# GpSimd makes three of the eight high parts of the activations in the gate

## The chip, the cores and the metric

The kernel runs on one core of one Trainium2 chip. The metric is the device time of one execution in microseconds. Engines are called PE (TensorE), DVE (VectorE), ACT (ScalarE), POOL (GpSimd) and SP (the queue that issues most DMAs).

## The reference

A graph network with two convolutions is followed by a mixture-of-experts layer over 6250 rows of 256 values. Only the second part matters here:

```
x = layernorm(x)
H = gelu(x @ W1 + b1)                       # 6250 x 1024
probs = softmax(H @ Wg + bg)                # 8 experts
assign = argmax(probs)
out = x_in + probs[e] * (H @ Wd[e] + bd[e]) # with e = assign, row by row
```

## The kernel before

The rows are cut into 49 tiles of 128, and two tiles make a pair. The work runs in stages with a barrier between them: sorting the edges, aggregation, two linear layers, aggregation again, the end of the graph network, then the **gate** and the **experts**. The gate computes H and the eight logits for each pair, picks an expert for each row, counts each row's place among those of its expert, and scatters the row to that place in a table in HBM. The experts stage reads the table back in order, computes H once more, and multiplies by the weights of the chosen expert.

Products are made in float16 with every operand split into a high and a low part. The 1024 hidden units are 8 chunks `h` of 128. In the gate every pair `i` (steps 0 to 24, the last with one tile) goes through this:

- PE (`pe_hidden`): six matmuls of 256 columns for each chunk, into one of four PSUM banks (`UB = 4`). Chunk `h` waits until the GELU of four chunks earlier has read the bank (`u.gelu`). After chunk 1 it transposes the rows of the next pair out of `stage`; after chunk 4 it makes the `ranks` of pair i-3, which wait for `s_slot` of pair i-4. After the eight chunks come the `logits` of pair i-1 (32 small matmuls).
- ACT (`act_hidden`): GELU of each chunk into `hf` (one buffer for the eight chunks, so the GELU of chunk `h` also waits until `h_lo` of that chunk of the pair before has been made, `u.split`). It makes the high part `h_hi` of chunks 0, 2, 3, 5 and 7, each one behind the GELU of the next chunk, and after `h_hi` of chunk 2 the high part of the next pair's transposed rows (`xt_hi`).
- DVE (`dve_hidden`): for chunks 1, 4 and 6 (`DVE_HIGH`) `h_hi` as well (L1920), and for all eight the low part `h_lo = hf * beta - h_hi` (L1925), in the order of the chunks. After chunk 0 comes `place` for pair i-4 (L2148 to L2153, gives `slot`), after chunk 3 `xt_lo` (L1907), which the next pair's first matmul waits for, and `choose` for pair i-2 (L2128 to L2139).
- POOL: for each i a copy of the pair's rows into `stage` (L2037), as soon as PE has transposed pair i-2 (`u.tr`), and then the two scatters (L2042) of pair i-6, as soon as DVE has placed it.

Steps 4 to 21 of PE, ACT and DVE run in a hardware loop of two steps; the others and all of POOL are written out. The order on each engine is that of the code; semaphores alone join the engines. After the last step DVE finishes the places of the last four pairs, works out which rows each tile of the experts stage has, and SP writes padding rows and the probabilities; then comes the barrier. `dve_hidden` serves the experts stage too.

Of the kernel before, what the change touches and what calls it, by code (L numbers as in the profile page):

```python
# [20 lines left out]
ALU = mybir.AluOpType  # L21
AX = mybir.AxisListType

P = 128
N, C, IC, HID, NEXP, NE = 6250, 256, 512, 1024, 8, 100000
EPS = 1e-5
NT = -(-N // P)
NP_ = NT * P
LAST = N - (NT - 1) * P
KC, KI, KH = C // P, IC // P, HID // P  # L30
# [220 lines left out]
def prepare(nc, m, a):  # L251
# [5 lines left out]
    EARLY = [(NBUILT + 6 * q, NBUILT + 6 * q + 6) for q in range(NADJ // 6)]  # L257
    LATE = [(0, 6), (6, 12), (12, NBUILT)]
    COUNTS = EARLY + LATE
    assert NADJ % 6 == 0 and NBUILT - 12 <= 7  # L260
# [1553 lines left out]
UB = 4  # L1814
DVE_HIGH = (1, 4, 6)
# [88 lines left out]
def dve_xt(dve, m, u, i, par, ntile):  # L1904
    i = i + u.first
    dve.wait_ge(u.xthi, i + 1)
    dve.tensor_tensor(m.xt_lo[:, par, :, 0:ntile * P],  # L1907
                      m.ps[:, TBANK, :].rearrange("p (k n) -> p k n", k=KC)[:, :, 0:ntile * P],
                      m.xt_hi[:, par, :, 0:ntile * P], ALU.subtract).then_inc(u.xt, 1)


def dve_hidden(dve, m, u, i, par, ntile, nxt, between={}):

    n = ntile * P
    i = i + u.first
    highs = 0
    for h in range(KH):
        if h in DVE_HIGH:
            dve.wait_ge(u.gelu, i * KH + (h + 1 + UB))
            dve.tensor_scalar(m.h_hi[:, par, h, 0:n], m.hf[:, h, 0:n], m.beta[:, h:h + 1], None, ALU.mult).then_inc(u.own, 1)  # L1920
            dve.wait_ge(u.own, i * len(DVE_HIGH) + (DVE_HIGH.index(h) + 1))
        else:
            highs += 1
            dve.wait_ge(u.hi, i * (KH - len(DVE_HIGH)) + highs)
        dve.scalar_tensor_tensor(m.h_lo[:, par, h, 0:n], m.hf[:, h, 0:n], m.beta[:, h:h + 1], m.h_hi[:, par, h, 0:n],  # L1925
                                 ALU.mult, ALU.subtract).then_inc(u.split, 1)
        if h == 3 and nxt:
            dve_xt(dve, m, u, i + 1 - u.first, 1 - par, nxt)
        if h in between:
            between[h]()  # L1930
# [19 lines left out]
def gate(nc, m, a):  # L1950

    rows = m.rows
# [8 lines left out]
    rk, slotf, slot = take("rk", [P, 2, NEXP], F32), take("slotf", [P, 2], F32), take("slot", [P, NT], I32)  # L1961
# [3 lines left out]
    stage = take("stage", [P, 2, 2, C], F32)  # L1965
# [6 lines left out]
    u = m.hidden  # L1972
# [8 lines left out]
    NPAIR = NT // 2  # L1981
    LB, RB = (5, 7), 6
    tiles = lambda i: 1 if i == NPAIR else 2
# [11 lines left out]
    with nc.Block() as block:  # L1995
        @block.sync
        def _(sp):
            for e in range(0, NEXP, 2):
                n = KH // 2
                sp.dma_start(m.wd[:, e:e + 2, :, :, :, :].rearrange("p e k h t c -> p (e k) (h t c)"),  # L2000
                             m.wd_dram[e * n:(e + 2) * n, :, :].rearrange("n p f -> p n f")).then_inc(m.s_wd, 16)
            sp.dma_start(m.bd[:, :, :].rearrange("p e c -> p (e c)"), bass.AP(a.fbd.tensor, 0, [[0, P], [1, NEXP * C]])).then_inc(m.s_bd, 16)
            sp.wait_ge(s_const, 8)
            sp.dma_start(m.sorted_rows[NEXP * REG:NEXP * REG + P, :], prow[:, :]).then_inc(s_padded, 16)
            sp.wait_ge(s_pads, 1)
            for e in range(NEXP):
                at = sp.value_load(padi[0:1, e:e + 1], min_val=e * REG, max_val=e * REG + NP_)
                sp.dma_start(m.sorted_rows[bass.ds(at, P), :], prow[:, :]).then_inc(s_padded, 16)
            sp.wait_ge(s_probS, 1)
            sp.dma_start(m.prob_dram.rearrange("(t p) c -> t (p c)", p=P), probT[:, :]).then_inc(m.s_prob, 16)  # L2010
            sp.wait_ge(s_padded, 16 * (NEXP + 1))

        @block.gpsimd
        def _(pool):
            pool.iota(rows[:, :, C].bitcast(I32), [[P, NT]], base=0, channel_multiplier=1).then_inc(s_const, 1)
            pool.memset(tri[:, :], 1.0).then_inc(s_init, 1)
            pool.memset(prow[:, :], 0.0).then_inc(s_init, 1)
            pool.memset(valid[:, :], 1.0).then_inc(s_init, 1)
            pool.wait_ge(s_init, 3)

            pool.affine_select(out=tri[:, :], in_=tri[:, :], compare_op=ALU.is_ge, fill=0.0,
                               base=-1, pattern=[[1, P]], channel_multiplier=-1).then_inc(s_const, 1)
            pool.affine_select(out=valid[:, :], in_=valid[:, :], compare_op=ALU.is_ge, fill=0.0,
                               base=LAST - 1, pattern=[[0, 1]], channel_multiplier=-1).then_inc(s_const, 1)
            pool.iota(prow[:, C:C + 1].bitcast(I32), [[0, 1]], base=N, channel_multiplier=0).then_inc(s_const, 1)
            pool.iota(prio[:, :], [[-1, NEXP]], base=NEXP, channel_multiplier=0, allow_small_or_imprecise_dtypes=True).then_inc(s_const, 1)
            for t in (run, m.reg_base):
                pool.iota(t[:, :], [[REG, NEXP]], base=0, channel_multiplier=0, allow_small_or_imprecise_dtypes=True).then_inc(s_const, 1)
            pool.iota(tv[:, :], [[1, 64]], base=0, channel_multiplier=0, allow_small_or_imprecise_dtypes=True).then_inc(s_const, 1)
            pool.wait_ge(s_const, 8)  # L2030
            LATE = 6
            for i in range(NPAIR + 1 + LATE):
                if i <= NPAIR:
                    n = tiles(i)
                    if i >= 2:
                        pool.wait_ge(u.tr, i - 1)
                    pool.tensor_copy(stage[:, i % 2, 0:n, :], rows[:, 2 * i:2 * i + n, 0:C]).then_inc(s_stage, 1)  # L2037
                if i >= LATE:
                    pool.wait_ge(s_slot, i - LATE + 1)
                    for t in range(2 * (i - LATE), 2 * (i - LATE) + tiles(i - LATE)):  # L2040
                        n = P if t < NT - 1 else LAST
                        pool.indirect_dma_start(m.sorted_rows, bass.IndirectOffsetOnAxis(ap=slot[:n, t:t + 1], axis=0),  # L2042
                                                rows[:n, t, :], None).then_inc(s_scat, 16)
            pool.wait_ge(s_scat, 16 * NT)

        @block.tensor
# [64 lines left out]
        def _(dve):  # L2111
# [29 lines left out]
            def place(dve, i, par, ntile):  # L2141
                t = slice(0, ntile)

                def lk(ins, n):
                    ins.then_inc(s_place, 1)
                    dve.wait_ge(s_place, i * 4 + n)
                dve.wait_ge(s_rk, i + 1)
                lk(dve.tensor_tensor(rk[:, t, :], m.ps[:, RB, 0:NEXP * ntile].rearrange("p (t e) -> p t e", e=NEXP),  # L2148
                                     run[:, :].unsqueeze(1).to_broadcast([P, ntile, NEXP]), ALU.add), 1)
                lk(dve.tensor_tensor(rk[:, t, :], rk[:, t, :], ohf[:, par, t, :], ALU.mult), 2)  # L2150
                lk(dve.tensor_tensor(run[:, :], run[:, :], m.ps[:, RB, 2 * NEXP:3 * NEXP], ALU.add), 3)
                lk(dve.tensor_reduce(slotf[:, t], rk[:, t, :], AX.X, ALU.add), 4)
                dve.tensor_copy(slot[:, bass.ds(2 * i, ntile)], slotf[:, t]).then_inc(s_slot, 1)  # L2153

            def step(dve, i, par, n):
                nxt = 0 if n == NPAIR else 1 if n == NPAIR - 1 else 2

                between = {}
                if n is None or n >= 4:
                    between[0] = lambda: place(dve, i - 4, par, 2)  # L2160
                if n is None or n >= 2:
                    between[3] = lambda: choose(dve, i - 2, par, 2)
                dve_hidden(dve, m, u, i, par, 1 if n == NPAIR else 2, nxt, between)
            dve_xt(dve, m, u, 0, 0, 2)
            steps(dve, step)
            for i in range(NPAIR - 3, NPAIR + 1):
                place(dve, i, i % 2, tiles(i))
# [208 lines left out]
```

## Time and profile before

| | us |
|---|---|
| median of 3 runs | 1857.0 |
| lowest and highest | 1855.56 and 1859.79 |
| time of the profiled execution | 1859.56 |
| its span in the profile | 1857.8 |
| gate, from its first POOL work to its last scatter | 1297 to 1515 |
| experts stage | from about 1525 |

The profile gives, for each engine, when each instruction ran and what ended the wait before it. The granted clock of PE is shown as a share of its full rate. "x3" means that three instructions are merged into one row, whose duration is that of all three; those of an engine overlap a little.

### The profile page before, as it was taken

How to read it: one execution, taken by the hardware profiler on the slowest of the kernel's cores; microseconds unless marked ns; L12 is line 12 of the kernel's file. 1: busy time of each engine (PE TensorE's matmuls, PEld its weight loads, DVE VectorE, ACT ScalarE, POOL GpSimd, SP SyncE). 2: the span in 40 equal slices, each digit the busy share in tenths (PEclk: the TensorE clock that was granted, in tenths of full speed). 3: DMA queues.
4: the chain of work that ended last, by engine and by line, in shares of the span. 5: the costliest groups of instructions: out<-in, count | busy, mean ns of one | idle time of the engine just before them, and what ended most of it. 6: DMA issues, size and time to landing. Idle time of an engine off the chain costs nothing. (4 is left out here: it accounts for less than half of the span.)

```text
span 1857.8 us, 36775 instructions
## 1 busy us (share of the span) xinstructions
PE 1579.0 (85%) x11153; PEld 1182.1 (64%) x11154; DVE 1178.6 (63%) x4511; ACT 971.2 (52%) x2001; POOL 936.2 (50%) x989
## 2 busy tenths in 40 slices
PE   0229999999999896989999999975888839999996
PEld 0215666666666696856656555655777728899995
DVE  6478888888886377932234344337788965656663
ACT  0555555555554355832334222228888837766773
POOL 5747677777777000047777777723133332333433
PEclk9999999999999897999999999989999969999998
DMA  8546566666666000478999999837500021111110
GB/s 248 164 138 214 193 208 208 209 208 208 209 208 208 12 0 32 148 260 309 299 314 313 336 321 313 291 122 231 195 34 34 32 75 33 48 47 46 48 47 15
DMA packets 152562, 305.72 MB, mean 165 GB/s; under 512 B 26099, under 2 KB 107989, under 8 KB 144638
## 3 DMA queue, kind: packets, MB, share of 16 engines
q1 hardware_dynamic: 104354, 191.99, 29.6%
q0 software_dynamic: 41744, 105.90, 18.1%
q10 hardware_dynamic: 6348, 6.40, 1.1%
q8 instruction: 58, 0.95, 0.2%
q14 instruction: 58, 0.48, 0.1%
HBM read 212.02 MB, written 99.68 MB: 168 GB/s over the span
## 5 line engine op out<-in xcount | busy, mean ns | idle before, releaser
L1165 POOL DMA_INDIRECT grows<-table_dram,gsrc x680 | 657.9, 967 | 337.3 <-issue 309.0
L1099 PE MATMUL ps<-table,adj 128*128 128x512 f16 x2842 | 707.1, 381 | 5.7 <-PEq L1466 5.7
L1099 PEld LDWEIGHTS ps<-table,adj 128*128 128x128 f16 x2842 | 389.7, 142 | 169.3 <-issue 12.1
L856 ACT ACTIVATE adj<-ps 128x490 f16<-128x490 f32 (+1 forms) x390 | 223.5, 573 | 182.3 <-PE ps L841 178.2
L1893 ACT ACTIVATE hf<-ps,b1f,unscale 128x256 f32<-128x256 f32 (+1 forms) x424 | 233.4, 562 | 119.6 <-PE ps L1864 95.8
L1864 PE MATMUL ps<-xt_hi,fw_parts 128*128 128x256 f16 (+1 forms) x1696 | 255.4, 274 | 5.5 <-DVE xt_lo L1907 5.3
L828 DVE TENSOR_SCALAR oh_k<-iota_k,keyrem 128x246 f16<-128x246 f16 x780 | 237.8, 309 | 0.0
L1925 DVE SCALAR_TENSOR_TENSOR h_lo<-hf,beta,h_hi 128x256 f16<-128x256 f32 (+1 forms) x424 | 190.1, 482 | 70.0 <-ACT h_hi L1888 64.3
L827 DVE TENSOR_SCALAR oh_r<-iota_r,keyrem 128x128 f16<-128x128 f16 x780 | 214.9, 278 | 26.6 <-PE ps L841 21.6
L1048 PE MATMUL ps<-grows,oh_g 128*128 128x512 f16 x680 | 167.1, 380 | 18.0 <-DMA grows<-table_dram,gsrc 18.0
L1864 PEld LDWEIGHTS ps<-xt_hi,fw_parts 128*128 128x128 f16 x1696 | 162.4, 98 | 26.2 <-DVE xt_lo L1907 5.4
L841 PE MATMUL ps<-oh_k,oh_r 128*128 128x245 f16 x780 | 148.7, 273 | 17.3 <-DVE oh_k L828 13.6
L1864 PE MATMUL ps<-xt_lo,fw_parts 128*128 128x256 f16 (+1 forms) x848 | 162.3, 273 | 0.0
L2276 PE MATMUL ps<-wd,h_hi 128*128 x896 | 148.4, 273 | 0.9 <-DVE y L2333 0.9
L841 PEld LDWEIGHTS ps<-oh_k,oh_r 128*128 128x128 f16 x780 | 75.6, 98 | 94.8 <-DVE oh_k L828 20.2
L1888 ACT ACTIVATE h_hi<-hf,beta 128x256 f16<-128x256 f32 (+1 forms) x265 | 133.0, 502 | 1.7
L920 DVE SCALAR_TENSOR_TENSOR tmp_d<-ps,disP,tmp_d 128x256 f32<-128x256 f32 x30 | 14.5, 484 | 186.6 <-ACT tmp_d L1124 186.6
L913 DVE TENSOR_SCALAR oh_g<-iota_r,gloc 128x128 f16<-128x128 f16 x680 | 125.7, 281 | 0.3
L1048 PEld LDWEIGHTS ps<-grows,oh_g 128*128 128x128 f16 x680 | 65.4, 98 | 93.3 <-DMA grows<-table_dram,gsrc 23.9
L2255 POOL DMA_INDIRECT out<-out_rows,in_rows x56 | 57.3, 1023 | 130.3 <-DVE out_rows L2337 121.8
L2276 PE MATMUL ps<-wd,h_lo 128*128 x448 | 122.1, 273 | 0.0
L2042 POOL DMA_INDIRECT sorted_rows<-rows,slot x49 | 48.5, 989 | 128.6 <-DVE slot L2153 121.0
(354 smaller groups left out, 2228.8 us busy)
## 6 DMA issues: line engine op xcount, KB each, us to landing
adj_dram<-adj SPq DMA_DIRECT2D x30, 1568.0 KB
adj<-adj_dram SPq DMA_DIRECT2D x30, 1568.0 KB, 8.2
cv_raw<-fwd SPq DMA_DIRECT2D x64, 256.0 KB, 5.5
table_dram<-table SPq DMA_DIRECT2D x14, 896.0 KB, 4.1
grows<-table_dram,gsrc POOLq DMA_INDIRECT x680
wd_dram<-cv_parts SPq DMA_DIRECT2D x32, 256.0 KB, 5.1
wd<-wd_dram SPq DMA_DIRECT2D x4, 2048.0 KB, 16.8
in_rows<-sorted_rows SPq DMA_DIRECT2D x56, 129.5 KB, 2.1
```

The costliest lines, as they stand in the source:

```text
L827: dve.tensor_scalar(a.oh_r[:, n % OHR, i, :], m.iota_r[:, :], m.keyrem[:, 1, j, w:w + 1], None, ALU.is_equal)
L828: last = dve.tensor_scalar(a.oh_k[:, n % OHR, i, :], m.iota_k[:, :], m.keyrem[:, 0, j, w:w + 1], None, ALU.is_equal)
L841: last = pe.matmul(m.ps[:, n % 3, at:at + keys], a.oh_r[:, n % OHR, i, :], a.oh_k[:, n % OHR, i, 0:keys], start=True, stop=True)
L856: act.activation(m.adj[:, q % 3, d0:d0 + wide, :].rearrange("r d c -> r (d c)"), m.ps[:, n % 3, 0:wide * NT], ACT.Copy).then_inc(a.s_adj, 1)
L1048: last = pe.matmul(acc, m.oh_g[:, n % GOR, j, :], m.grows[:, n % GR, j, :], start=False, stop=part == PT - 1 and j == PARTS[part] - 1)
L1099: last = pe.matmul(acc, adj[:, :, c], table[:, c, :], start=c == 0, stop=c == NT - 1)
L1165: pool.indirect_dma_start(m.grows[:, n % GR, j, :], None, m.table_dram, bass.IndirectOffsetOnAxis(ap=m.gsrc[:, g, part * BT + j:part * BT ...
L1864: last = pe.matmul(m.ps[:, h % UB, 0:n], m.w1[:, 2 * k + half, w, at:at + P], x[:, par, k, 0:n], start=q == 0 and k == 0, stop=q == 2 and ...
L1888: act.activation(m.h_hi[:, par, h, 0:n], m.hf[:, h, 0:n], ACT.Copy, scale=m.beta[:, h:h + 1]).then_inc(u.hi, 1)
L1893: act.activation(m.hf[:, h, 0:n], m.ps[:, h % UB, 0:n], ACT.Gelu, bias=m.b1f[:, h:h + 1], scale=m.unscale[:, 0:1]).then_inc(u.gelu, 1)
L1925: dve.scalar_tensor_tensor(m.h_lo[:, par, h, 0:n], m.hf[:, h, 0:n], m.beta[:, h:h + 1], m.h_hi[:, par, h, 0:n], ALU.mult, ALU.subtract).th ...
L2276: last = pe.matmul(m.ps[:, DB + j, 0:C], h[:, par, k, j * P:(j + 1) * P], w, start=q == 0 and k == 0, stop=q == 2 and k == KH - 1)
```

## The change

DVE no longer makes `h_hi` of chunks 1, 4 and 6 in the gate. POOL makes them, with the same instruction, and raises the same semaphore `u.own` that DVE's `h_lo` already waits on. POOL's order becomes, for step i: high part of chunk 1, first scatter of pair i-6, high part of chunk 4, second scatter, high part of chunk 6, copy of the rows of pair i+2. Each high part waits for its GELU and for the logits of pair i-2 (`u.done`), whose buffer it overwrites. The copies no longer wait for `u.tr` when they are the first two, and those of pair i+2 come behind step i's last high part. After step 24 POOL has the scatters of pairs 19 to 24 left. The experts stage is unchanged.

```diff
-def dve_hidden(dve, m, u, i, par, ntile, nxt, between={}):
+def dve_hidden(dve, m, u, i, par, ntile, nxt, between={}, pool_high=False):
...
         if h in DVE_HIGH:
-            dve.wait_ge(u.gelu, i * KH + (h + 1 + UB))
-            dve.tensor_scalar(m.h_hi[:, par, h, 0:n], m.hf[:, h, 0:n], m.beta[:, h:h + 1], None, ALU.mult).then_inc(u.own, 1)
+            if not pool_high:
+                dve.wait_ge(u.gelu, i * KH + (h + 1 + UB))
+                dve.tensor_scalar(m.h_hi[:, par, h, 0:n], m.hf[:, h, 0:n], m.beta[:, h:h + 1], None, ALU.mult).then_inc(u.own, 1)
             dve.wait_ge(u.own, i * len(DVE_HIGH) + (DVE_HIGH.index(h) + 1))
...
+            def copy(i):
+                n = tiles(i)
+                if i >= 2:
+                    pool.wait_ge(u.tr, i - 1)
+                pool.tensor_copy(stage[:, i % 2, 0:n, :], rows[:, 2 * i:2 * i + n, 0:C]).then_inc(s_stage, 1)
+
+            def high(i, h):
+                n = tiles(i) * P
+                pool.wait_ge(u.gelu, i * KH + (h + 1 + UB))
+                pool.wait_ge(u.done, i + 1)
+                pool.tensor_scalar(m.h_hi[:, i % 2, h, 0:n], m.hf[:, h, 0:n], m.beta[:, h:h + 1], None, ALU.mult).then_inc(u.own, 1)
+
+            def scatter(t):
+                n = P if t < NT - 1 else LAST
+                pool.indirect_dma_start(m.sorted_rows, bass.IndirectOffsetOnAxis(ap=slot[:n, t:t + 1], axis=0),
+                                        rows[:n, t, :], None).then_inc(s_scat, 16)
+
+            for i in range(2):
+                copy(i)
             for i in range(NPAIR + 1 + LATE):
-                if i <= NPAIR:
-                    n = tiles(i)
-                    if i >= 2:
-                        pool.wait_ge(u.tr, i - 1)
-                    pool.tensor_copy(stage[:, i % 2, 0:n, :], rows[:, 2 * i:2 * i + n, 0:C]).then_inc(s_stage, 1)
-                if i >= LATE:
-                    pool.wait_ge(s_slot, i - LATE + 1)
-                    for t in range(2 * (i - LATE), 2 * (i - LATE) + tiles(i - LATE)):
-                        n = P if t < NT - 1 else LAST
-                        pool.indirect_dma_start(...).then_inc(s_scat, 16)
+                for k in range(len(DVE_HIGH)):
+                    if i <= NPAIR:
+                        high(i, DVE_HIGH[k])
+                    if i >= LATE and k < tiles(i - LATE):
+                        pool.wait_ge(s_slot, i - LATE + 1)
+                        scatter(2 * (i - LATE) + k)
+                if i + 2 <= NPAIR:
+                    copy(i + 2)
```

## Rows read from the trace of the kernel before

**Rows 1.** Busy us (count) of PE, PEld, DVE, ACT, POOL, and clock, in one stretch.

```profile
1345.55:1476.37 130.82, 109.61 (x1430) 96.31 (x1428) 116.70 (x417) 109.32 (x224) 41.19 (x49) 1.00 0.09 33
```

**Rows 2.** Waits in that stretch: who for whom, total us, times, longest.

```profile
PE ps L2066 <- DVE slot L2153: 23.1, 17, 1.9
```

**Rows 3.** DVE in order of time, one pair.

```profile
1401.36 0.17 DVE L2148 TENSOR_TENSOR rk<-ps,run 128x16 f32<-128x16 f32 x1
...
1402.28 0.17 DVE L2153 CAST slot<-slotf 128x2 f32 x1
1402.41 0.35 DVE L1920 TENSOR_SCALAR h_hi<-hf,beta 128x256 f16<-128x256 f32 x1
1402.80 1.28 DVE L1925 SCALAR_TENSOR_TENSOR h_lo<-hf,beta,h_hi 128x256 f16<-128x256 f32 x3
1403.99 0.68 DVE L1907 TENSOR_TENSOR xt_lo<-ps,xt_hi 128x512 f16<-128x512 f32 x1
...
1405.33 0.33 DVE L2131 TENSOR_TENSOR now<-now,mx 128x16 f32<-128x16 f32 x1
...
1409.60 0.17 DVE L2148 TENSOR_TENSOR rk<-ps,run 128x16 f32<-128x16 f32 x1
```

**Rows 4.** ACT in order of time, the same pair and the next.

```profile
1403.58 1.14 ACT L1893 ACTIVATE hf<-ps,b1f,unscale 128x256 f32<-128x256 f32 x2 [0.42 <-PE ps L1864]
...
1406.35 1.22 ACT L1893 ACTIVATE hf<-ps,b1f,unscale 128x256 f32<-128x256 f32 x2 [0.24 <-PE ps L1864]
1407.47 0.50 ACT L1888 ACTIVATE h_hi<-hf,beta 128x256 f16<-128x256 f32 x1
...
1410.54 0.51 ACT L1888 ACTIVATE h_hi<-hf,beta 128x256 f16<-128x256 f32 x1
```

**Rows 5.** PE in order of time: the ranks, and the next transposes.

```profile
1402.51 0.18 PE L2066 MATMUL ps<-oh,tri 128*128 128x8 f16 x1 [1.11 <-DVE slot L2153]
...
1406.73 0.60 PE L1850 MATMUL ps<-id,stage 128*128 128x128 f32 x4
```

**Rows 6.** POOL in order of time, scatters of the first and last pair of the stretch.

```profile
1345.55 0.99 POOL L2042 DMA_INDIRECT sorted_rows<-rows,slot  x1 [5.59 <-DVE slot L2153]
1346.84 0.96 POOL L2042 DMA_INDIRECT sorted_rows<-rows,slot  x1 [0.30 <-issue]
...
1476.37 0.98 POOL L2042 DMA_INDIRECT sorted_rows<-rows,slot  x1 [5.36 <-DVE slot L2153]
```

**Rows 7.** POOL's groups by line and shape, whole span (busy us, mean ns, idle).

```profile
L1598 POOL TENSOR_TENSOR rs<-ve,mh 128x4 f32<-128x4 f32 x12 | 12.1, 1006 | 38.8 <-DVE ve L1637 38.8
L380 POOL CAST words<-dst_i 100x1024 int16<-100x1024 int32 x1 | 1.3, 1317 | 3.6 <-DMA dst_i<-dst 3.6
L2037 POOL COPY stage<-rows 128x256 f32<-128x256 f32 x1 | 0.4, 409 | 0.0
```

**Rows 8.** POOL in order of time, two copies near the gate's start.

```profile
1312.53 0.79 POOL L2037 COPY stage<-rows 128x512 f32<-128x512 f32 x1 [7.08 <-PE ps L1850]
...
1326.02 0.61 POOL L2037 COPY stage<-rows 128x512 f32<-128x512 f32 x1 [5.96 <-PE ps L1850]
```

**Rows 9.** DVE in order of time around those two copies.

```profile
1311.97 0.88 DVE L1925 SCALAR_TENSOR_TENSOR h_lo<-hf,beta,h_hi 128x256 f16<-128x256 f32 x2
...
1326.11 1.19 DVE L1925 SCALAR_TENSOR_TENSOR h_lo<-hf,beta,h_hi 128x256 f16<-128x256 f32 x2
```

**Rows 10.** DVE in order of time: places of steps 4 and 24, the last high part.

```profile
1335.57 0.17 DVE L2148 TENSOR_TENSOR rk<-ps,run 128x16 f32<-128x16 f32 x1
...
1497.87 0.17 DVE L2148 TENSOR_TENSOR rk<-ps,run 128x16 f32<-128x16 f32 x1
...
1502.74 0.28 DVE L1920 TENSOR_SCALAR h_hi<-hf,beta 128x128 f16<-128x128 f32 x1
```

**Rows 11.** POOL's last scatter of the gate.

```profile
1513.11 1.57 POOL L2042 DMA_INDIRECT sorted_rows<-rows,slot  x1 [0.31 <-issue]
```

**Rows 12.** SP's queue at the gate's end, the padding rows.

```profile
1512.69 9.34 SPq L2008 DMA_DIRECT2D sorted_rows<-prow  x8
```

More of the change, by code:

```diff
@@ L2031, in _ @@
             LATE = 6
-            for i in range(NPAIR + 1 + LATE):
-                if i <= NPAIR:
-                    n = tiles(i)
-                    if i >= 2:
-                        pool.wait_ge(u.tr, i - 1)
-                    pool.tensor_copy(stage[:, i % 2, 0:n, :], rows[:, 2 * i:2 * i + n, 0:C]).then_inc(s_stage, 1)
-                if i >= LATE:
-                    pool.wait_ge(s_slot, i - LATE + 1)
-                    for t in range(2 * (i - LATE), 2 * (i - LATE) + tiles(i - LATE)):
-                        n = P if t < NT - 1 else LAST
-                        pool.indirect_dma_start(m.sorted_rows, bass.IndirectOffsetOnAxis(ap=slot[:n, t:t + 1], axis=0),
-                                                rows[:n, t, :], None).then_inc(s_scat, 16)
+            def copy(i):
[14 more added lines that the diff above has]
+                copy(i)
+            for i in range(NPAIR + 1 + LATE):
+                for k in range(len(DVE_HIGH)):
[6 more added lines that the diff above has]
+                    copy(i + 2)
             pool.wait_ge(s_scat, 16 * NT)
@@ L2162, in step @@
                     between[3] = lambda: choose(dve, i - 2, par, 2)
-                dve_hidden(dve, m, u, i, par, 1 if n == NPAIR else 2, nxt, between)
+                dve_hidden(dve, m, u, i, par, 1 if n == NPAIR else 2, nxt, between, pool_high=True)
             dve_xt(dve, m, u, 0, 0, 2)
```

## Prediction

> **What bounds the kernel now.** The change touches the gate alone, so I looked first for what sets the length of a step there. The view of busy time by stretch, over the regular part of the gate, is the start. DVE is busy 116.7 of 130.82 us, ACT and PE 109 each, POOL 41 [rows 1]. The stretch runs from the first scatter of one pair to that of the pair 16 later, so a step takes 130.82 / 16 = 8.18 us [rows 6]. PE's granted clock is 1.00 in it, the 2.4 GHz level.
>
> The view of waits says who is late: PE waits 17 times, 23.1 us in all, for DVE's `slot` before its ranks [rows 2]. ACT's waits are for PE's chunks behind these ranks: it stands 0.42 and 0.24 us in one step [rows 4]. DVE's own order of time then shows one pair from `place` to `place`, 1401.36 to 1409.60, 8.24 us, in which it waits for no other engine's data [rows 3]. The reader is to see that DVE is the engine that everything else follows here. POOL has 5.4 to 5.6 us in each step in which it waits for `slot` [rows 6], so it has time for more.
>
> **What the change removes.** One `h_hi` on DVE takes from 1402.41 to the start of the next instruction at 1402.80, 0.39 us [rows 3]. Three a step are 1.17 us. DVE's own step without them is 8.24 - 1.17 = 7.07 us.
>
> That isn't yet the new step, since loops through several engines come next. I work them out from the same pair:
>
> - The ranks loop. Ranks at 1402.51 on PE [rows 5]; PE's chunks 5 to 7, logits and chunks 0 and 1 follow, and the GELU of the next chunk 1 ends at 1406.35 + 1.22 = 1407.57, 5.06 us on. ACT's `h_hi` of chunk 0 ends at 1407.97, 0.40 later [rows 4]. Then on DVE `h_lo` of chunk 0, 0.40 with some 0.08 of signalling (three take 1402.80 to 1403.99), and `place`, 1401.36 to 1402.45, 1.09 [rows 3], and 0.06 to the next ranks. The sum is 7.09 us a step.
> - The longer loop, over two steps. Up to that GELU again 5.06. ACT then ends `h_hi` of chunk 3 at 1411.05, 3.48 us on [rows 4]. DVE does `h_lo` of chunk 3, 0.48 with the signalling, and from `xt_lo` at 1403.99 to the next `place` at 1409.60 another 5.61, of which the change removes 2 x 0.39, so 4.83. `place` and the way to the ranks are 1.15 [rows 3]. The sum is 5.06 + 3.48 + 0.48 + 4.83 + 1.15 = 15.00 us, 7.50 a step.
>
> So without any cost of POOL's new work the step would be 7.50 us, not 7.07.
>
> **What POOL's work costs.** No row shows this instruction on POOL. The nearest one is POOL's copy of 128x256 f32, 409 ns: the same elements, one tensor read. The cast of 1024 int32 took 1317 ns, 1.3 ns an element with all of its fixed cost; 256 elements at that and a fixed 0.2 us are 0.53. The dearest row of an arithmetic operation there is 1006 ns, for four elements, which is a power and not a product [rows 7]. I take 0.41 us, keep 0.41 below and 1.0 above; it is nearest to the copy. POOL's step is then 3 x 0.41 + 2 x 0.97 + 0.30 + 0.62 = 4.1 us of 7.5, and 5.9 with the upper price. Its time hides beside the others unless one of its results is late:
>
> - The high parts. That of chunk 1 starts when the GELU of chunk 1 is done, as ACT's of chunk 0 does, and DVE has `h_lo` of chunk 0 and the whole `place` to do before it needs it. Those of 4 and 6 start while DVE is still at chunk 3, `xt_lo` and `choose`. A scatter ahead of one holds it up by at most 0.97 + 0.30. Covered; if the cover were gone, it would cost DVE up to 1.3 us a step.
> - The copy for pair i+2, behind the high part of chunk 6. The GELU of chunk 6 ends at 1403.58 + 1.14 = 1404.72 [rows 4] and PE comes to the transposes at 1406.73 [rows 5], 2.0 us later. High part and copy take 0.41 + 0.62 = 1.03, with signals and the end of a scatter up to 1.6. Covered by 0.4 us; with the price of 1.0 it is late by about 0.2. Pairs 2 and 3 lose the early copies they have now; I put down 0.3 us in all for the filling of the pipeline.
> - The scatters. They move two steps later and no longer wait for `slot`. After POOL's last high part (DVE's was at 1502.74 [rows 10]) 11 are left, 11 x 1.27 = 14.0 us, so they end near 1517.1 on the old axis, where the last now ends at 1514.7 [rows 11]. SP's eight padding rows last until 1522.0 [rows 12]. Hidden, with 4.9 us for the last rows to land.
>
> **What the two engines cost each other.** A copy on POOL began at 1326.02, `h_lo` on DVE at 1326.11, and two `h_lo` took 1.19 us where two took 0.88 at 1311.97 [rows 8, 9]: DVE stood 0.31 us, until 0.40 after the copy's start. The copy that began behind a running `h_lo` at 1312.53 took 0.79 in place of 0.61 [rows 8]. In `choose`, `now` took 0.33 beside a copy [rows 3]. So the one that comes second stands. The copy has 512 elements and held DVE for 0.40; a high part has 256, so 0.20 by an estimate from those rows. `h_lo` is eight times 0.40 us of a step. I take it that three high parts and the moved copy hold DVE for some 0.3 us more in two steps of the longer loop (between none and 4 x 0.2 a step), 0.15 a step. The step is 7.65 us.
>
> The Trainium skill (page "SBUF — State Buffer", section "Who interferes with whom") says that a VectorE instruction with two SBUF inputs and a GpSimd instruction that reads SBUF exclude each other, and that the second is blocked until the first is done. That speaks against this change, since `h_lo` reads `hf` and `h_hi`. The trace agrees that DVE stands, but for 0.40 us of a copy that is 0.61 long, not for all of it [rows 8, 9]. By the rule as it stands each high part could cost DVE its full 0.41, three 1.23 against the 1.17 removed, and the time would be 1857 in place of the 1847 below.
>
> **The sum.** The steps that shorten are those between the places of steps 4 and 24: 1335.57 to 1497.87, 20 steps, 8.115 us on average [rows 10]. They save 20 x (8.115 - 7.65) = 9.3 us. Step 24's three high parts of 128 columns (0.28 each) leave DVE's path too, 0.8, less 0.1 of standing. Start of the pipeline: -0.3. Together 9.7 us. Against the profiled execution that is 1859.56 - 9.7 = 1849.9; the median of the runs shown is 2.6 below it, so 1857.0 - 9.7 = 1847.3, say **1847**.
>
> **The rivals.**
> - The ranks loop alone bounds (7.1 us a step): the longer loop overlaps better than I lay it out, and POOL's reads fall where DVE reads PSUM. For it speaks that POOL's high part of chunk 1 runs beside ACT's of chunk 0, when DVE mostly waits. 20 x 1.0 + 0.7 = 20.7 us: 1836.
> - No change: each high part holds DVE as long as it was there itself, 3 x 0.39, because nearly every one meets a running `h_lo` and the handing over costs as much again as the reading. The work has then only moved: 1857. The rule of "SBUF — State Buffer" in the Trainium skill would end here too. Against it stands the 0.40 of a copy twice as long.
> - Slower, by one mechanism: POOL's product is dear (1.0 us, which the power in rows 7 allows). Less the fixed 0.2 us it then holds DVE for 0.8, 2.4 a step if all three meet `h_lo`. With half of them the step is 7.50 + 1.2 = 8.7, 20 x (8.7 - 8.115) = 12 us more in all: 1869. The point from which it decides: DVE stands more than 8.115 - 7.50 = 0.6 us a step longer in the longer loop, or 0.2 for each high part with every one meeting `h_lo`.
> - The change doesn't free DVE since `h_lo` of chunks 1, 4, 6 now waits for POOL in place of doing the work: possible if DVE keeps up with ACT closely; same size as no change, and taken with it.
>
> **How the numbers follow.** Forecast (step 7.4 to 7.9, 1842 to 1852): 0.55. Ranks loop alone, around 1836: 0.13. Between forecast and no change, and no change, 1853 to 1861: 0.18. Slower: 0.14. A measurement of this kernel tells apart 0.2%, 3.7 us, so faster below 1853.3: 0.55 + 0.13 + a part of the third case, 0.04 = 0.72; same 0.14; slower 0.14. The range leaves out the top of the slow case and the best of the fast one: 1836 to 1859.
>
> **What would show it.** Right: no L1920 on DVE before 1500, 75 new ones on POOL near 0.41 us; scatters apart by 7.65 us; PE's wait for `slot` smaller than 1.1 us a step; some `h_lo` longer than 0.48 beside POOL's instructions; copies ended before PE asks, no wait of the transposes for `stage`; scatters after the last step back to back and no wait of SP or the experts for them. Wrong: POOL's high part above 0.6 us, DVE waiting for `h_hi` of POOL, or PE's transposes waiting for POOL.

## The result, and the profile after

The changed kernel takes 1852.22 us (median of 8 runs, 1850.44 to 1858.72), the kernel before, measured beside it, 1859.76 us. The ratio is 0.9967 with a 95% interval of 0.9953 to 0.9982: 0.33%, some 6 us, with between 3.3 and 8.7 us possible. The two medians lie 7.5 us apart, inside that interval; one of the eight runs of the kernel before took 5939.86 us, and the ratio leaves it out. The forecast was 9.7 us, outside the interval. The direction was right and 1852 lies in the range, but the size was forecast too large. Of the 5.2 us between 1847 and 1852.2, 2.8 have nothing to do with the change: the kernel before itself took 1859.76 us beside the changed one, and not the 1857.0 that the forecast started from.

The profiled execution took 1853.08 us, 6.5 less than the 1859.56 of before. Where they went is read from five times in each trace: the first instruction of the gate on VectorE (the `memset` of `ones`), the places of step 4, of step 24 and the last, and SyncE's first load of the next stage, the experts.

| stretch, us | before | after | difference | forecast |
|---|---|---|---|---|
| gate's start to place of step 4 | 39.04 | 39.29 | +0.25 | +0.3 |
| 20 steps | 162.30 | 153.90 | -8.4 | -9.3 |
| step 24 to the last place | 12.79 | 12.33 | -0.46 | -0.7 |
| last place to the experts' first load | 14.60 | 17.22 | **+2.6** | 0 |
| gate in all | 228.73 | 222.74 | -6.0 | -9.7 |

What lies outside the gate differs by -0.5 us and is no part of the change. So the steps and step 24 came out near the forecast, and the term that stood at nothing cost 2.6 us. The start's +0.25 can't be told from nothing: two more traces of the changed kernel have 39.0 and 38.6 us there, and a second trace with the gate of before (price, below) has 39.3.

VectorE in order of time, around the places of steps 4 and 24 [rows 10] and the last:

```profile
1336.24 0.16 DVE L2166 TENSOR_TENSOR rk<-ps,run 128x16 f32<-128x16 f32 x1
...
1490.14 0.16 DVE L2166 TENSOR_TENSOR rk<-ps,run 128x16 f32<-128x16 f32 x1
...
1502.47 0.17 DVE L2166 TENSOR_TENSOR rk<-ps,run 128x8 f32<-128x8 f32 x1 [0.38 <-PE ps L2089]
```

(1490.14 - 1336.24) / 20 = 7.695 us a step, where it was 8.115. Away from the loop's ends, over the 14 steps in its middle, it is 7.80 where it was 8.18; I call that the regular step.

Busy time in the regular part (the columns of [rows 1], a slightly shorter stretch), and its waits (total, times, longest; [rows 2]):

```profile
1345.55:1470.00 124.45, 111.10 (x1422) 95.15 (x1420) 108.92 (x368) 109.21 (x224) 93.59 (x95) 1.00 0.09 32
```

```profile
PE ps L2084 <- DVE slot L2171: 13.1, 16, 1.0
...
ACT hf L1893 <- PE ps L1864: 6.7, 24, 0.4
DVE h_lo L1926 <- ACT h_hi L1888: 4.2, 15, 0.6
...
PEld ps L1850 <- POOL stage L2038: 2.4, 8, 0.3
```

VectorE is no longer alone at the top: PE has 89% of the stretch, ACT and VectorE 88% each, where it was 84% for PE and ACT and 89% for VectorE. PE's wait for `slot` fell from 1.4 us a time to 0.8. VectorE now waits for ACT's `h_hi` of chunk 3, the link of the longer loop. And POOL went from 31% to 75% busy, 5.9 us a step where the forecast had 4.1. Its groups by shape say why (busy us, mean ns, idle before), against [rows 7]:

```profile
L2044 POOL TENSOR_SCALAR h_hi<-hf,beta 128x256 f16<-128x256 f32 x72 | 77.0, 1069 | 56.0 <-ACT hf L1893 55.1
...
L2048 POOL DMA_INDIRECT sorted_rows<-rows,slot x49 | 50.7, 1035 | 9.8 <-issue 8.8 <-DVE slot L2171 0.9
```

The product takes 1.07 us on average, not 0.41. POOL and VectorE in order of time show what it does to its neighbour ([rows 3] has VectorE's before). In `choose`, `now` is the logits less their greatest, `lg` a copy of that, and `sc` and `ohf` mark the expert that is picked:

```profile
1400.10 0.92 POOL L2044 TENSOR_SCALAR h_hi<-hf,beta 128x256 f16<-128x256 f32 x1 [0.38 <-ACT hf L1893]
...
1402.26 0.94 POOL L2044 TENSOR_SCALAR h_hi<-hf,beta 128x256 f16<-128x256 f32 x1
1403.14 0.60 POOL L2038 COPY stage<-rows 128x512 f32<-128x512 f32 x1
1404.55 1.35 POOL L2044 TENSOR_SCALAR h_hi<-hf,beta 128x256 f16<-128x256 f32 x1 [0.80 <-ACT hf L1893]
```

```profile
1400.42 0.48 DVE L1926 SCALAR_TENSOR_TENSOR h_lo<-hf,beta,h_hi 128x256 f16<-128x256 f32 x1 [0.26 <-ACT h_hi L1888]
...
1402.16 0.17 DVE L2149 TENSOR_TENSOR now<-now,mx 128x16 f32<-128x16 f32 x1
1402.59 0.64 DVE L2151 COPY lg<-now 128x16 f32 x1 [0.26 <-DVE now L2149]
1403.11 0.16 DVE L2152 SCALAR_TENSOR_TENSOR sc<-now,prio 128x16 f32<-128x16 f32 x1
...
1403.51 0.27 DVE L2154 TENSOR_TENSOR ohf<-sc,best 128x16 f32<-128x16 f32 x1
...
1403.92 2.21 DVE L1926 SCALAR_TENSOR_TENSOR h_lo<-hf,beta,h_hi 128x256 f16<-128x256 f32 x5
1406.05 0.16 DVE L2166 TENSOR_TENSOR rk<-ps,run 128x16 f32<-128x16 f32 x1
...
1410.49 0.59 DVE L2152 SCALAR_TENSOR_TENSOR sc<-now,prio 128x16 f32<-128x16 f32 x1
```

POOL's high part of chunk 6 (1402.26 to 1403.20) falls into `choose`. The copy `lg`, 0.17 us long elsewhere, takes 0.64 and ends at 1403.23, just as POOL is done; one step on it is `sc` that takes 0.59. The high part of chunk 1 comes second, behind a running `h_lo`, and there POOL is the one that is held up: 1.35 us in place of 0.92. The high part of chunk 4 (1400.10 to 1401.02) has a whole `h_lo` of VectorE beside it (1400.42 to 1400.90), and neither is longer than elsewhere, 0.92 and 0.48. So the same instruction has three outcomes in one step, by where it falls.

The end of the gate is a block's end: every engine drains its queues and then all meet at a barrier. SyncE's and POOL's rows there (how long in ns, when), before and then after:

```profile
L1995 POOLq DRAIN  x1: 4071/4071/4071, 1519.9 to 1519.9; - x1
...
L1995 SPq DRAIN  x1: 7/7/7, 1524.1 to 1524.1; - x1
L1995 SPq EVENT_SEMAPHORE  x1: 17/17/17, 1524.3 to 1524.3; - x1
```

```profile
L1996 POOLq DRAIN  x1: 4071/4071/4071, 1514.5 to 1514.5; - x1
...
L1996 SPq DRAIN  x1: 7/7/7, 1516.2 to 1516.2; - x1
L1996 SPq EVENT_SEMAPHORE  x1: 17/17/17, 1518.7 to 1518.7; - x1
```

Before, POOL's drain ended at 1519.9 + 4.07 = 1523.97 and SyncE was ready at 1524.1: a tie. After, SyncE is ready at 1516.2 and all wait for POOL until 1518.6. The last scatters [rows 11, 12] in the changed kernel:

```profile
1507.48 1.57 POOL L2048 DMA_INDIRECT sorted_rows<-rows,slot  x1 [0.30 <-issue]
```

```profile
1504.42 9.84 SPq L2009 DMA_DIRECT2D sorted_rows<-prow  x8
```

The last place came 8.2 us earlier and the last scatter only 5.6. From its end at 1509.05 to the drain's start are 5.4 us for its rows to land, and 4.07 more for the drain: 9.5 us in which the forecast counted 4.9.

### The profile page after: what moved, and what is told of

Read it like the earlier page. It is cut to its first block and busy times, and to the rows that moved or that the text cites. A ratio compares the mean times of both kernels' runs of the same rounds, so it can differ in the third digit from the quotient of the medians.

```text
span 1851.3 us, 36796 instructions
## 1 busy us (share of the span) xinstructions
PE 1586.4 (86%) x11153; PEld 1184.4 (64%) x11154; DVE 1165.9 (63%) x4436; ACT 971.2 (52%) x2001; POOL 1015.1 (55%) x1064
## 5 line engine op out<-in xcount | busy, mean ns | idle before, releaser
L2044 POOL TENSOR_SCALAR h_hi<-hf,beta 128x256 f16<-128x256 f32 (+1 forms) x75 | 79.6, 1062 | 56.9 <-ACT hf L1893 56.0
```

## The experiments

Three questions: what the product costs by itself and what of that reaches the step; which instructions stand for which; and whether the end really costs 2.6 us. Most kernels were timed against the kernel before on the same chip. All regular steps, and "last place to load", are from the traces, as above. The regular step repeats well: three traces of the changed kernel have 7.80, 7.80 and 7.81, three with the scatters a step nearer 7.80 each, the two of act6 7.59 and 7.58.

| kernel | regular step | last place to load | ratio to before |
|---|---|---|---|
| before | 8.18 | 14.60 | 1 |
| changed | 7.80 | 17.22 | 0.9967 (0.9953 to 0.9982) |
| plain_copy | 7.74 | 17.81 | 0.9949 (0.9929 to 0.9968) |
| none_made | 7.51 | 16.59 | 0.9927 (0.9905 to 0.9948) |
| moved_only | 8.04 | 16.32 | 1.0013 (0.9992 to 1.0034) |
| two_tensors | 8.01 | 16.49 | 1.0028 (0.9981 to 1.0074) |
| late5 | 7.80 | 15.44 | 0.9971 (0.9926 to 1.0016) |
| copy_first | 7.86 | 17.85 | 0.9971 (0.9923 to 1.0019) |
| both14 | 7.82 | 14.74 | 1.0010 (0.9968 to 1.0051) |
| no_read | 7.62 | 18.02 | one run, 2118.8 beside 2131.0 |
| act6 | 7.59 | 14.69 | 0.9946 (0.9910 to 0.9982) |
| after_again (changed) | 7.80 | 17.70 | 0.9983 (0.9948 to 1.0017) |
| late5_again | 7.80 | 16.04 | 0.9941 (0.9908 to 0.9973) |
| after_third (changed) | 7.81 | 17.47 | 0.9966 (0.9953 to 0.9979) |
| late5_third | 7.80 | 14.91 | 0.9967 (0.9954 to 0.9980) |
| act6_again | 7.58 | 14.52 | 0.9922 (0.9904 to 0.9939) |

two_tensors to both14, and then no_read, act6, after_again and late5_again, ran where the stages ahead of the gate took far longer (the kernel before 2121 us beside the first four and 2131 us beside the others). The gate's own steps are comparable, the ratios of these are loose. "Last place to load" is less so: in all of them SyncE came to the barrier after POOL (in after_again 16.6 us after the last place against POOL's 16.2, in late5_again 14.9 against 13.3), so there it doesn't show POOL's drain.

**price**: the kernel before, with single instructions on POOL behind its scatters, each waited for, nothing beside them.

```diff
             pool.wait_ge(s_scat, 16 * NT)
+            pool.wait_ge(u.tr, NPAIR + 1)
+            pool.wait_ge(s_probS, 1)
+            for n in (128, 256, 512):
+                alone(pool.tensor_copy(to32, src))
+                alone(pool.tensor_copy(to16, src))
+                alone(pool.tensor_scalar(to32, src, m.beta[:, 1:2], None, ALU.mult))
+                alone(pool.tensor_scalar(to16, src, m.beta[:, 1:2], None, ALU.mult))
+                alone(pool.tensor_scalar(to16, src, 0.5, None, ALU.mult))
+            alone(pool.tensor_tensor(low[:, 1, 0, 0:256], src, m.beta[:, 1:2].to_broadcast([P, 256]), ALU.mult))
```

> The kernel before, with 16 added instructions on GpSimd at the end of the gate, one at a time with nothing beside them; they write buffers that nobody reads any more. They give the price of a product by a column of scalars and of its neighbours. Theory A (the product itself is dear on GpSimd): the product of 128x256 f32 to f16 takes 0.85 to 0.95 us alone, twice the copy's 0.41. Theory B (it takes the copy's 0.41 alone, and in the gate it is stretched by VectorE's reads of two tensors): 0.41 to 0.5 us alone. The time of the whole is of no interest here; it should be some 10 us above the kernel before.

POOL in order of time:

```profile
1525.26 0.53 POOL L2063 TENSOR_SCALAR stage<-rows 128x128 f16<-128x128 f32 x1
1525.85 0.40 POOL L2059 COPY stage<-rows 128x256 f32<-128x256 f32 x1
1526.31 0.40 POOL L2060 CAST stage<-rows 128x256 f16<-128x256 f32 x1
...
1527.83 0.92 POOL L2062 TENSOR_SCALAR stage<-rows,beta 128x256 f16<-128x256 f32 x1
1528.84 0.85 POOL L2063 TENSOR_SCALAR stage<-rows 128x256 f16<-128x256 f32 x1
...
1532.79 1.56 POOL L2062 TENSOR_SCALAR stage<-rows,beta 128x512 f16<-128x512 f32 x1
...
1536.01 0.61 POOL L2065 TENSOR_TENSOR stage<-rows,beta 128x256 f16<-128x256 f32 x1
```

The product of 128x256 takes 0.92 us with nothing beside it, the copy and the cast 0.40. From 256 to 512 elements it grows by 0.64, that is 2.5 ns an element, where the copy has 0.8. The type written makes no difference, the column of scalars 0.07. The same product written with two tensors takes 0.61. The price of 0.41 was too small by more than twice, and most of it, 0.92 of the 1.07, is the instruction itself and not its neighbour.

**plain_copy**: POOL's high part is a plain cast of `hf`; `beta` is left out of it. **none_made**: POOL makes no high part at all, it only raises the semaphore; `h_hi` of chunks 1, 4 and 6 stays at the zero written once at the start.

```diff
 # plain_copy
-                pool.tensor_scalar(m.h_hi[:, i % 2, h, 0:n], m.hf[:, h, 0:n], m.beta[:, h:h + 1], None, ALU.mult).then_inc(u.own, 1)
+                pool.tensor_copy(m.h_hi[:, i % 2, h, 0:n], m.hf[:, h, 0:n]).then_inc(u.own, 1)
 # none_made
-                pool.tensor_scalar(m.h_hi[:, i % 2, h, 0:n], m.hf[:, h, 0:n], m.beta[:, h:h + 1], None, ALU.mult).then_inc(u.own, 1)
+                pool.sem_inc(u.own, 1)
```

> The changed kernel with a copy to f16 in place of GpSimd's product; the factor beta is left out of the high parts of chunks 1, 4 and 6, everything else is as it was. If the dear product is what keeps the gate's step at 7.8 us (theory A), each of GpSimd's high parts takes 0.41 to 0.5 us, the step falls to the forecast's 7.65 or below and the time by 3 to 5 us against the changed kernel, to 1848. If the loops through TensorE and ScalarE set the step (theory B), it stays at 7.8 us and the time at 1852.

> The changed kernel in which nobody makes the high parts of chunks 1, 4 and 6 (they are left out; the buffer is zeroed once). GpSimd only raises the semaphore at the same points. This is the floor of the change. By the forecast's longer loop the step is 7.50 us, by its ranks loop alone 7.1 us. Theory A (the product's price): 7.3 to 7.5 us a step, 6 to 10 us below the changed kernel, about 1844. Theory B (other loops set it): 7.7 to 7.8 us, at most 2 us below.

none_made has the step without any cost of POOL's product: 7.51 us, where the forecast's longer loop summed to 7.50. That fits the two-step loop as the bound that takes over, and the net price of POOL's three products is 7.80 - 7.51 = 0.29 us a step, 0.58 in one turn of the loop. VectorE's rows of none_made:

```profile
1430.58 0.30 DVE L2152 TENSOR_TENSOR now<-now,mx 128x16 f32<-128x16 f32 x1
1431.14 0.17 DVE L2154 COPY lg<-now 128x16 f32 x1 [0.26 <-DVE now L2152]
...
1431.94 2.07 DVE L1926 SCALAR_TENSOR_TENSOR h_lo<-hf,beta,h_hi 128x256 f16<-128x256 f32 x5
```

Against the changed kernel's pair above, `lg` is shorter by 0.47, `ohf` by 0.1 and the five `h_lo` by 0.14, and `now` is longer by 0.13, since POOL's copy of rows now falls beside it: 0.58 us in the end. In the next step, where `sc` stood and `now` takes 0.51, the same count gives some 0.3, so the rows account for the 0.58 in one step of two. So 7.51 isn't free of POOL either: the copy still holds `now` there, as it did in the kernel before (0.33, [rows 3]). In plain_copy the product is 0.4 to 0.5 us and the step 7.74: half the price gives back only 0.06 us. POOL's copy of rows then falls where the product fell (1433.37 to 1433.98), and VectorE stands for it:

```profile
1433.42 0.60 DVE L2149 TENSOR_TENSOR now<-now,mx 128x16 f32<-128x16 f32 x1
...
1435.07 2.21 DVE L1926 SCALAR_TENSOR_TENSOR h_lo<-hf,beta,h_hi 128x256 f16<-128x256 f32 x5
```

**moved_only**: VectorE makes all high parts as before; POOL keeps the changed order and its waits, without the product.

```diff
                 pool.wait_ge(u.done, i + 1)
-                pool.tensor_scalar(m.h_hi[:, i % 2, h, 0:n], m.hf[:, h, 0:n], m.beta[:, h:h + 1], None, ALU.mult).then_inc(u.own, 1)
+                return
...
-                dve_hidden(dve, m, u, i, par, 1 if n == NPAIR else 2, nxt, between, pool_high=True)
+                dve_hidden(dve, m, u, i, par, 1 if n == NPAIR else 2, nxt, between)
```

> The changed kernel's order of waits, scatters and copies on GpSimd, but VectorE makes all its high parts as before and GpSimd makes none. If the moved order is free (the forecast's step for it), the gate's step is 8.1 to 8.2 us and the time that of the kernel before, 1858 within 2 us. If the later copies or scatters cost something, it is slower than before by that; if the earlier copies of before cost VectorE time in its choice of experts, it is faster by up to 20 x 0.15 = 3 us.

The order alone shortens the regular step by 0.14 us and lengthens the end by 1.7; the time is that of before (1.0013, 0.9992 to 1.0034). So of the 0.38 us that the changed kernel's step is shorter, 0.14 come from the order and 0.24 from moving the products. In the kernel before, `now` took 0.33 us beside the copy of rows; here the copy begins 0.1 to 0.2 us earlier against `place` and is nearly done when `now` begins. `now` here, and then the barrier, where POOL is last again, by 1.3 us:

```profile
1405.82 0.18 DVE L2149 TENSOR_TENSOR now<-now,mx 128x16 f32<-128x16 f32 x1
```

```profile
L1996 POOLq DRAIN  x1: 4071/4071/4071, 1520.9 to 1520.9; - x1
...
L1996 SPq DRAIN  x1: 7/7/7, 1523.7 to 1523.7; - x1
L1996 SPq EVENT_SEMAPHORE  x1: 17/17/17, 1525.2 to 1525.2; - x1
```

So 1.7 of the 2.6 us come with the moved order alone, and none_made, again without a product, loses 2.0. The last scatter begins 2.4 us after the last place in the kernel before, 3.8 in moved_only, 4.4 in none_made and 5.0 in the changed kernel.

**two_tensors**: the same product as an operation with two tensors, 0.61 us by price.

```diff
-                pool.tensor_scalar(m.h_hi[:, i % 2, h, 0:n], m.hf[:, h, 0:n], m.beta[:, h:h + 1], None, ALU.mult).then_inc(u.own, 1)
+                pool.tensor_tensor(m.h_hi[:, i % 2, h, 0:n], m.hf[:, h, 0:n], m.beta[:, h:h + 1].to_broadcast([P, n]), ALU.mult).then_inc(u.own, 1)
```

> The changed kernel with GpSimd's product written as a product of two tensors, beta spread over the columns; the results are the same. Alone that took 0.61 us where the product by a column of scalars took 0.92. If the length of the product decides what VectorE loses (theory A), the wait in the choice of experts falls by the 0.3 us, the gate's step from 7.80 to between 7.74 (the step with plain copies) and 7.79, and the time by 0.5 to 1.2 us. If it is the encounter and not the length (theory B), nothing changes beyond 0.02 us a step. If two tensors read on GpSimd hold the port more than one does (theory C), h_lo gets longer and the step exceeds 7.80.

It is a third shorter and makes the step 0.2 us longer, 8.01. POOL, then VectorE:

```profile
1682.28 0.61 POOL L2038 COPY stage<-rows 128x512 f32<-128x512 f32 x1
1684.32 0.62 POOL L2044 TENSOR_TENSOR h_hi<-hf,beta 128x256 f16<-128x256 f32 x1 [1.43 <-ACT hf L1893]
```

```profile
1682.06 0.88 DVE L2149 TENSOR_TENSOR now<-now,mx 128x16 f32<-128x16 f32 x1
...
1683.99 2.43 DVE L1926 SCALAR_TENSOR_TENSOR h_lo<-hf,beta,h_hi 128x256 f16<-128x256 f32 x5
```

The high part of chunk 1 begins behind running `h_lo`, as in the changed kernel, but isn't held up: 0.62 us. VectorE's five take 2.43 us in place of 2.21, and one `now` 0.88 beside high part and copy in a row. In this form POOL goes first and VectorE stands. Which engine yields depends on the instruction, and counts for more than the instruction's length.

**no_read**: POOL writes zeros in place of the product and reads nothing (0.31 us); the high parts are left out.

```diff
+                pool.memset(m.h_hi[:, i % 2, h, 0:n], 0.0).then_inc(u.own, 1)
```

> The changed kernel with a memset in place of GpSimd's product: it writes the same places and reads nothing, the high parts of chunks 1, 4 and 6 are zeros. Theory A (VectorE stands because GpSimd reads): h_lo and the choice's instructions with two inputs take their own times beside it, five h_lo 2.07 us as where GpSimd makes none, step 7.51 to 7.60. Theory B (any work of GpSimd at that time delays VectorE): step near the 7.74 of the plain copies.

```profile
1702.31 0.31 POOL L2044 MEMSET h_hi<- 128x256 f16 x1 [1.45 <-ACT hf L1893]
```

```profile
1700.39 0.51 DVE L2149 TENSOR_TENSOR now<-now,mx 128x16 f32<-128x16 f32 x1
...
1701.96 2.07 DVE L1926 SCALAR_TENSOR_TENSOR h_lo<-hf,beta,h_hi 128x256 f16<-128x256 f32 x5
```

The five `h_lo` take 2.07 us beside it, as with nothing made, and the step is 7.62. The plain cast, 0.55 us beside the same five, made them 2.21, so it is POOL's reading that holds them up. The step lies just above the 7.51 to 7.60 expected. What still stands is `now`, beside POOL's copy of rows, which reads.

**copy_first**: POOL copies the next rows ahead of the high part of chunk 6.

```diff
+                    if k == 2 and i + 2 <= NPAIR:
+                        copy(i + 2)
                     if i <= NPAIR:
                         high(i, DVE_HIGH[k])
...
-                if i + 2 <= NPAIR:
-                    copy(i + 2)
```

> The changed kernel with the copy of the rows of pair i+2 ahead of GpSimd's high part of chunk 6 and not behind it. TensorE's waits for stage (0.3 us in every second step) should go. If they are part of what sets the step (theory A), it falls by up to 0.15 us, 3 us in all. If VectorE's chain through the choice of experts sets it (theory B), they are slack, and the later high part of chunk 6 moves VectorE's standing to other instructions: step between 7.75 and 7.95.

PE's waits for `stage` are gone and the step is 7.86, no shorter. But VectorE's standing has moved as well: `now` takes 0.73 us in one step and 0.40 in the next, `lg` and `sc` their own times again. That the 0.3 us in every second step were slack fits this and isn't shown by it alone.

**both14**: POOL makes chunks 1 and 4, VectorE chunk 6 again, with a semaphore of its own for POOL's.

```diff
+POOL_HIGH = (1, 4)
...
-            if not pool_high:
+            if not pool_high or h not in POOL_HIGH:
```

> GpSimd makes the high parts of chunks 1 and 4 alone, and VectorE that of chunk 6 again. In the changed kernel the high part of chunk 6 falls into the choice of experts and holds VectorE for 0.45 to 0.6 us there. Theory A (that standing is a cost as large as the 0.39 us that it frees): step 7.70 to 7.80, the time equal to the changed kernel's within 2 us. Theory B (GpSimd's work of chunk 6 is nearly free): VectorE's own 0.39 us comes back in the loop of two steps, 0.2 a step, 7.95 to 8.0, 4 us slower.

The regular step is 7.82, as with three. Taking chunk 6 off VectorE gave it 0.39 us, and its product on POOL took as much back in `choose`. At the gate's end its trace has one gap of 5.6 us on VectorE that belongs to no instruction of the edit (act6 has one of 2.7, act6_again none); its ratio, 1.0010 (0.9968 to 1.0051), is too loose to say more than the step does.

**late5**, and twice more beside the changed kernel itself, **after_again** with **late5_again** and **after_third** with **late5_third**: the scatters come one step nearer to their pair.

```diff
-            LATE = 6
+            LATE = 5
```

> The changed kernel with the scatters five steps behind in place of six, so that 9 are left after the last step in place of 11. Theory A (the scatters at the end hold up the barrier): GpSimd's last scatter starts 2.5 us earlier against the last place, the first load of the experts stage comes 2.4 us earlier, and the time falls by 2.4 us to 1850; the step stays at 7.80. Theory B (the barrier waits for SP's rows and probabilities, as the forecast had it): nothing changes.

> The changed kernel once more, unchanged, on the same chip as the next two, so that they can be compared with it. Its gate should again last about 6 us less than that of the kernel before, with a step of 7.80 us.

> The scatters five steps behind in place of six, with nothing else changed, timed in more rounds and beside the changed kernel. Theory A (in the changed kernel GpSimd's last scatters and the draining of its queue behind them close the gate, 2.4 us after all others): 2.4 to 3 us below the changed kernel, and some 9 us below the kernel before, which is what the forecast had with the scatters hidden. Theory B (the difference seen in the first trace of it was chance): the same time as the changed kernel.

> The changed kernel, unchanged, as the measure for the next two on the same chip. If the chip's DMAs run at the speed of the first profile, its gate ends on GpSimd's queue: SP is ready at the barrier 2.4 us before GpSimd, and the first load comes 17.2 us after the last place.

> Scatters five steps behind in place of six. Theory A (the scatters end the gate): the first load comes 14.6 to 15.4 us after the last place as in the kernel before, 2 to 2.5 us below the changed kernel. Theory B (it is within the spread of the start and end of the stages): no difference. On a chip with slow DMAs SP ends the gate in both and there is no difference either, which then says nothing.

The barrier of late5_third:

```profile
L1996 POOLq DRAIN  x1: 4071/4071/4071, 1514.4 to 1514.4; - x1
...
L1996 SPq DRAIN  x1: 7/7/7, 1519.0 to 1519.0; - x1
L1996 SPq EVENT_SEMAPHORE  x1: 17/17/17, 1519.1 to 1519.1; - x1
```

POOL is done at 1518.5, ahead of SyncE's 1519.0: the tie is back. From last place to load it is 14.91 us against 17.47 in after_third, and the gate 219.17 against 222.17. The times don't show it: 1854.79 against 1854.93 us, ratios to before of 0.9967 and 0.9966, each uncertain by 0.0013. On the other chip the pair had 0.9941 (0.9908 to 0.9973) against 0.9983 (0.9948 to 1.0017), with SyncE last in both gates. In the profiled executions of the third pair, 1855.85 and 1854.79 us, the account closes: the gate of late5_third is 3.0 us shorter and began 2.1 us later, after stages that the edit doesn't touch. So a gain of 3 us at the gate's end is shown in the traces, and no gain of the whole is shown by the clock.

**act6, act6_again**: both14, with chunk 6's high part on ACT in place of VectorE, and the scatters as in late5.

```diff
-        if h in DVE_HIGH:
+        if h in DVE_HIGH and not (six and h == 6):
...
-        act.activation(m.h_hi[:, par, h, 0:n], m.hf[:, h, 0:n], ACT.Copy, scale=m.beta[:, h:h + 1]).then_inc(u.hi, 1)
+        act.activation(m.h_hi[:, par, h, 0:n], m.hf[:, h, 0:n], ACT.Copy, scale=m.beta[:, h:h + 1]).then_inc(m.s_six if h == 6 else u.hi, 1)
```

> GpSimd makes the high parts of chunks 1 and 4, ScalarE that of chunk 6, and the scatters are five steps behind. Theory A (what is left above the floor of 7.51 us is VectorE standing at the port in its choice of experts, because of GpSimd's high part of chunk 6): VectorE gets back 0.5 to 0.6 us in two steps, ScalarE's 0.40 us goes into waits that it has; step 7.55 to 7.70, 2 to 5 us below late5. Theory B (ScalarE's loop through the ranks takes the place: 7.09 + 0.40 = 7.49 plus the standing that is left): 7.8 or above, no faster.

> GpSimd makes chunks 1 and 4, ScalarE chunk 6, scatters five steps behind. Its step was 7.59 us against 7.80 in the first trace. Theory A: 20 x 0.21 = 4.2 us below late5, and 12 to 14 us below the kernel before. Theory B: the shorter step is lost at the gate's end, and it is within 1 us of late5.

The busy times of its regular part:

```profile
1354.00:1460.00 106.00, 96.07 (x1250) 84.42 (x1248) 91.03 (x323) 98.39 (x211) 68.73 (x71) 1.00 0.10 35
```

ACT takes on a sixth high part and becomes the busiest engine, 98.39 of 106.00 us, and the step falls to 7.58. With the end repaired the gate takes 213.79 us, 14.9 less than before. The time is 1843.36 us against 1860.57 before, ratio 0.9922 (0.9904 to 0.9939). Its interval doesn't meet that of the changed kernel on the same chip. This is the best version found. Its median is also 11.4 us below late5_third's, where 4.2 were expected: the two gates differ by 5.4, and in its trace the gate began 6.7 us earlier, after stages that no edit here touches. So not all of the 11.4 is the edit's.

## Why the prediction was right in direction and too large in size

- **What bounds, and what takes over: right as far as shown, with some luck in the number.** VectorE bounded the step, and behind it the two-step loop through PE, GELU, ACT's `h_hi` of chunk 3, `choose` and `place`, at 7.50 us. With no product made it is 7.51; both hold a `now` that stands beside the copy of rows. That loop was worked out for a step in the middle, but the sum took it from 8.115, the mean of 20 steps with the shorter ones at the ends. On that mean the changed kernel has 7.695 and none_made 7.42: the floor was 0.08 us a step too high (1.6 us of the sum), the standing 0.12 too low (2.4), and the two errors partly cancel. The ranks loop alone, the first rival (7.1), is excluded by none_made.
- **The price of POOL's product: wrong.** Taken at 0.41 us, "nearest to the copy"; it is 0.92 alone and 1.07 in the gate. The upper bound of 1.0 held the first and not quite the second, and it met the sign that I had named for a wrong forecast ("high part above 0.6 us"). It cost little: halving it (plain_copy) moves the step by 0.06. POOL's time is mostly hidden; at its upper price the forecast had POOL's step at 5.9 us, as measured.
- **What the two engines cost each other: too small by half.** Forecast 0.15 us a step, measured 0.29. The moved copy was counted as a further cost, and the moved order by itself turned out a gain: moved_only's step is 0.14 shorter than before. I scaled the copy's 0.40 down to 0.20 by its elements, and the product's 0.94 us held `lg` until its very end. In sum 20 steps saved 8.4 us and not 9.3.
- **The rival with the dear product: right in the price, wrong in its effect.** At 1.07 us it should have made the step 8.7. But the high part of chunk 1, which meets running `h_lo`, is itself held up and costs VectorE 0.14 us, that of chunk 4 costs it nothing, and only the one that falls into `choose` holds it for half of its length.
- **The end, the step that failed:** "Hidden, with 4.9 us for the last rows to land". The last scatter came 2.6 us later against the last place, as worked out there (2.4). What stands behind it is 5.4 us of landing and POOL's drain of 4.07 before the barrier. Before, that chain ended 0.1 us ahead of SyncE's, and so had no room at all. The trace of before held this row; the forecast went by SyncE's queue, and not by what each engine does between its last transfer and the barrier. 2.6 of the 3.7 us that the gate fell short are here, 0.9 are in the steps, and 0.2 in step 24.
- **Small terms.** The start's 0.3 us was 0.25, which is luck: the traces scatter by more. The transposes do wait for the moved copy, 0.3 us in every second step, where I had it covered by 0.4 and late by 0.2 at the price of 1.0. That was another of the signs of a wrong forecast; taking the wait away gained nothing (copy_first).

The Trainium skill ("SBUF — State Buffer", "Who interferes with whom") says that of a VectorE instruction with two SBUF inputs and a GpSimd instruction that reads SBUF the second is blocked until the first is finished, and that issue order decides who blocks. For the product in `choose` the trace agrees: `lg` and `sc` end with it, 0.47 and 0.42 us late, and my estimate of 0.20 was the worse guide. `lg` is a copy and reads only one tensor; it stands all the same. It agrees also that only a reading POOL instruction holds `h_lo` up (2.07 us beside the `memset`, 2.21 beside the product). It doesn't agree for the product of chunk 4, inside which an `h_lo` ran its 0.48 us with neither of them longer, nor for two_tensors, where POOL came behind running `h_lo` and was not held up, 0.62 us against 0.61 alone.

What stays open: why VectorE yields to the one form of the product and POOL to the other, why the product of chunk 4 and the `h_lo` inside it don't meet at all, whether a run that breaks the two-step loop would confirm it as the bound, and whether the 3 us at the gate's end reach the whole time, which no timing here resolves.

## What to carry to other kernels

Before calling a moved transfer hidden, follow it to the barrier: issue, landing, and the drain of the queue it is in, for each engine, and see which is last now; a tie hides a loss that the next delay makes real. When work goes to POOL, measure that very instruction by itself, and choose where it falls beside VectorE by what is on the critical loop there, since a shorter form can cost more. And let the traces say which engine has room once the old bound is gone: here taking chunk 6 from VectorE was worth nothing on POOL (7.82 to 7.80 us) and 0.2 us a step on ACT (7.82 to 7.58).

## What the runs showed of the hardware

- A product of 128x256 by a column of scalars takes 0.92 us on POOL, a copy or cast 0.40, the same product as a two-tensor operation 0.61 (price).
- POOL's queue drain at the end of the gate took 4.07 us in each of the four traces shown, after the last rows had landed. It is this block's figure: at the ends of other blocks in the trace of before it took from 0.04 to 22.5 us.
- POOL's scalar product is held up behind running `h_lo` of VectorE (0.92 to 1.35 and 1.53 us), its two-tensor form is not, and VectorE's five `h_lo` then take 2.43 us in place of 2.07. The scalar product with one `h_lo` inside it, and pauses around that, left both at 0.92 and 0.48 us.
